# A transformer block with routed experts: where the experts' steps that no tile fills stand

## The reference

```python
logits = einsum('bsh,eh->bse', h, gate_w) + expert_bias
weights = softmax(logits)
top_w, top_i = top_k(weights, 2)
top_w = top_w / (sum(top_w) + 1e-6)
for e in range(8):
    g = gelu(einsum('bsh,ih->bsi', h, w_up[e]))     # 256 -> 1024
    y = einsum('bsi,hi->bsh', g, w_down[e])         # 1024 -> 256
    out = out + sparse_w[..., e:e + 1] * y
out = layernorm(out) + h
x = x + gb * out
```

## Time and profile before

| | |
|---|---|
| median of three runs | 1329.73 us |
| profiled execution | 1329.79 us, span 1328.1 us |
| busy in the span: PE, DVE, ACT, POOL | 1115.8, 795.6, 643.0, 867.1 us |
| share of the chain that ended last: PE, issue, DVE, DMA, POOL | 30%, 2%, 2%, 1%, 1% |
| DMA queue of SP and ACT | 137.59 MB, 37.8% of 16 engines |
| DMA queue of POOL | 28.11 MB, 11.3% of 16 engines |

### The profile page before, as it was taken

One profiled execution on the slowest core, in us unless ns is written; L12 is line 12 of the kernel. 1 busy time (PEld: TensorE's weight loads), 2 busy tenths in 40 slices (PEclk: granted clock), 3 DMA queues, 4 the chain that ended last, 5 costly groups with the idle time before them and its releaser, 6 DMA issues. The chain is left out here.

```text
span 1328.1 us, 30712 instructions
## 1 busy us (share of the span) xinstructions
PE 1115.8 (84%) x11290; PEld 889.4 (67%) x11291; DVE 795.6 (60%) x2048; ACT 643.0 (48%) x913; POOL 867.1 (65%) x959
## 2 busy tenths in 40 slices
PE   4569999998999989989899813699999999999900
PEld 3346776777777767767677611588888888888800
DVE  4445668567685676756868359455555555555557
ACT  3447776775767767767677402122222222222212
POOL 2266597676875777758855437566666666666656
PEclk9779999999999999999999855799999999999965
DMA  8778674753548526564361245134344344242364
GB/s 289 205 204 182 219 180 116 177 125 102 150 113 200 126 97 144 136 173 136 91 128 65 96 159 159 33 50 110 57 98 110 45 110 110 47 107 48 45 161 131
DMA packets 122892, 167.14 MB, mean 126 GB/s; under 512 B 13048, under 2 KB 99320, under 8 KB 122784
## 3 DMA queue, kind: packets, MB, share of 16 engines
q1 hardware_dynamic: 103200, 137.59, 37.8%
q0 software_dynamic: 19584, 28.11, 11.3%
HBM read 105.22 MB, written 60.44 MB: 125 GB/s over the span
## 5 line engine op out<-in xcount | busy, mean ns | idle before, releaser
L927 DVE CUSTOM_DVE_ANT_0 b_sn<-b_ps_s,s_tile 128x512 f32<-128x512 f32 x512 | 341.5, 688 | 202.6 <-PE b_ps_s L1056 199.5
L869 ACT ACTIVATE b_pt<-b_ps_t 128x1024 f32<-128x1024 f32 x256 | 259.5, 1017 | 89.1 <-PE b_ps_t L1070 89.1
L1070 PE MATMUL b_ps_t<-s_ident,b_sn 128*128 128x128 f32 x2048 | 274.3, 277 | 9.8 <-POOL b_sn L760 8.1
L1070 PEld LDWEIGHTS b_ps_t<-s_ident,b_sn 128*128 128x128 f32 x2048 | 243.3, 143 | 48.1 <-issue 19.0
L760 POOL TENSOR_SCALAR b_sn<-b_sn,b_mn 128x512 f32<-128x512 f32 x256 | 175.3, 696 | 116.5 <-DVE b_mn L927 115.5
L1656 ACT ACTIVATE d_g<-d_ps_u 128x512 f32<-128x512 f32 x156 | 92.7, 598 | 315.1 <-PE d_ps_u L1769 308.6
L861 ACT ACTIVATE b_sn<-b_sn,b_mn 128x512 f32<-128x512 f32 x256 | 182.4, 721 | 101.1 <-DVE b_mn L927 94.1
L1056 PE MATMUL b_ps_s<-s_ks,s_qs 96*128 96x512 bf16 x512 | 181.9, 391 | 27.4 <-DVE b_mn L927 20.5
L1769 PE MATMUL d_ps_u<-d_xp,k_wu 128*128 128x256 bf16 x1776 | 201.9, 274 | 0.0
L1784 PE MATMUL d_ps_y<-k_wd,d_gp 128*128 128x256 bf16 x1776 | 199.9, 273 | 0.0
L1769 PEld LDWEIGHTS d_ps_u<-d_xp,k_wu 128*128 128x128 bf16 x1776 | 173.7, 98 | 21.7 <-issue 0.2
(11 more groups left out here) (198 smaller groups left out, 1219.7 us busy)
## 6 DMA issues: line engine op xcount, KB each, us to landing
w_parts<-b_w_split SPq DMA_DIRECT2D x32, 512.0 KB, 3.6
splits<-s_parts SPq DMA_DIRECT2D x32, 384.0 KB, 3.2
s_qs<-splits SPq DMA_DIRECT2D x96, 128.0 KB, 6.0
s_ks<-splits SPq DMA_DIRECT2D x96, 128.0 KB, 7.6
b_w_raw<-in_w_up_t SPq DMA_DIRECT2D x16, 512.0 KB, 10.6
b_w_raw<-in_w_down_t SPq DMA_DIRECT2D x16, 512.0 KB, 6.9
k_wu<-w_parts SPq DMA_DIRECT2D x8, 1024.0 KB
k_wd<-w_parts SPq DMA_DIRECT2D x8, 1024.0 KB
```

The lines of the kernel that those rows point to most:

```text
L869: act.activation(pt[:, m, 2 * pair:2 * pair + 2, :], ps_t[:, 2 * pair:2 * pair + 2, :], ACT.Exp).then_inc(exped, 1)
L927: dve.tensor_tensor_reduce(sn[:, n % 2, t, :], ps_s[:, t % 2, :], ahead.tile[:, n, at:at + S], -1.0, BIG, ALU.add, ALU.min, mn[:, n % 2, t ...
L1070: mm = pe.transpose(ps_t[:, j, t * P:(t + 1) * P], sn[:, m, t, j * P:(j + 1) * P], ident[:, :])
```

## The change

A turn is five steps. The first turns end in an empty step each, until there are no empty steps left; after that the filled ones go on without a gap. `empty` is 39 less the filled tiles. A place moves up by 256 for each empty step ahead of it: its tile divided by four (`STRIDE - 1`), at most `empty`. The same is done for `kept.filled`; the tables of slot and count of loads are looked up by the step less the empty steps before it, and a step is marked as empty where it is the fifth of a turn whose number is under `empty`. SP now waits for the scatters of all 39 steps before it reads the sums. In `up` TensorE waits, bank by bank, for gelu of the step before, which an empty step in between no longer covers.

```diff
+STRIDE = 5
+TURNS = -(-TABLE // STRIDE)
...
+            pool.iota(ints[:, AT_TURN:AT_MARK], pattern=[[1, TURNS], [0, STRIDE]], base=0, channel_multiplier=0).then_inc(pool_step, 1)
+            pool.iota(ints[:, AT_MARK:], pattern=[[1, TURNS], [-100, STRIDE]], base=100 * (STRIDE - 1), channel_multiplier=0).then_inc(pool_step, 1)
...
             rows = kept.rows[:, :, :].rearrange("p k t -> p (k t)")
+            turn = ((STRIDE - 1) * ROWS).bit_length() - 1
+            dve.tensor_scalar(empty[:, :], filled[:, NE - 1:NE], -1.0, float(RUN_TILES), ALU.mult, ALU.add)
+            link(dve.tensor_scalar(turn_u[:, 0:2 * NT], rows, turn, None, ALU.logical_shift_right))
+            link(dve.tensor_copy(turn_f[:, 0:2 * NT], turn_u[:, 0:2 * NT]))
+            link(dve.tensor_scalar(turn_f[:, 0:2 * NT], turn_f[:, 0:2 * NT], empty[:, :], float(ROWS), ALU.min, ALU.mult))
+            link(dve.tensor_tensor(turn_f[:, 0:2 * NT], turn_f[:, 0:2 * NT], places[:, :, :].rearrange("p k t -> p (k t)"), ALU.add))
+            link(dve.tensor_copy(rows, turn_f[:, 0:2 * NT]))
...
-            dve.tensor_scalar(kept.scattered[:, :], filled[:, NE - 1:NE], 16.0 * TT, None, ALU.mult)
-            link(dve.tensor_scalar(kept.filled[:, :], filled[:, :], 1.0, None, ALU.add))
+            of_expert = slice(2 * NT, 2 * NT + NE)
+            link(dve.tensor_copy(filled_u[:, :], filled[:, :]))
+            link(dve.tensor_scalar(turn_u[:, of_expert], filled_u[:, :], (STRIDE - 1).bit_length() - 1, None, ALU.logical_shift_right))
+            link(dve.tensor_copy(turn_f[:, of_expert], turn_u[:, of_expert]))
+            link(dve.tensor_scalar(turn_f[:, of_expert], turn_f[:, of_expert], empty[:, :], 1.0, ALU.min, ALU.add))
+            dve.tensor_tensor(kept.filled[:, :], filled[:, :], turn_f[:, of_expert], ALU.add)
             link(dve.tensor_scalar(last_tile[:, :], filled[:, NE - 1:NE], -1.0, None, ALU.add))
-            link(dve.tensor_scalar(index[:, :], iota_t, last_tile[:, :], None, ALU.min))
+            link(dve.tensor_scalar(index[:, :], turns, empty[:, :], None, ALU.min))
+            link(dve.tensor_tensor(index[:, :], iota_t, index[:, :], ALU.subtract))
+            link(dve.tensor_scalar(index[:, :], index[:, :], last_tile[:, :], None, ALU.min))
...
-            link(dve.tensor_scalar(scaled[:, :, 0], iota_t, last_tile[:, :], float(SPARE), ALU.is_gt, ALU.mult))
+            link(dve.tensor_scalar(scaled[:, :, 0], marks, empty[:, :], float(SPARE), ALU.is_lt, ALU.mult))
...
-            sp.wait_ge(y_out, sp.value_load(kept.scattered[0:1, 0:1], min_val=16, max_val=16 * TT * MAX_TILES))
+            sp.wait_ge(y_out, 16 * TT * RUN_TILES)
...
                 pe.wait_ge(kept.w_ready[slot], loaded)
                 for j in range(NIC):
+                    if j % 2 == 0:
+
+                        at_least(pe, gelued, (t - 1) * BANKS + j // 2 + 1)
```

More of the change, by code:

```diff
@@ L1207 @@
 SPARE = 2
+STRIDE = 5
+TURNS = -(-TABLE // STRIDE)
+assert (2 * STEPS - 1) // (STRIDE - 1) >= NE - 1
 SLOT, LOADED = range(2)
@@ L1231, in __init__ @@
         self.places = sb("places", [P, TABLE, 2, TT], U32)
-        self.scattered = sb("scattered", [P, 1], I32)
         self.tiles = sb("tiles", [P, 2, TABLE], I32)
@@ L1256, in route @@
         up_to = sb("up_to", [P, NE, NE])
-        ints = sb("ints", [P, NE + STEPS + TABLE + P], I32)
-        nums = sb("nums", [P, NE + STEPS + TABLE + P])
+        CONSTS = NE + STEPS + TABLE + P + 2 * TURNS * STRIDE
+        ints = sb("ints", [P, CONSTS], I32)
+        nums = sb("nums", [P, CONSTS])
         swing = sb("swing", [P, NE])
@@ L1277, in route @@
         last_tile = sb("last_tile", [P, 1])
+        empty = sb("empty", [P, 1])
+        turn_u = sb("turn_u", [P, 2 * NT + NE], U32)
+        turn_f = sb("turn_f", [P, 2 * NT + NE])
+        filled_u = sb("filled_u", [P, NE], U32)
         index = sb("index", [P, TABLE])
@@ L1293, in route @@
         ps_r = ctx.enter_context(nc.psum_tensor("c_ps_r", [P, 2, NT, 2 * NE], F32))
-        iota_e, steps, iota_t, iota_p = (nums[:, 0:NE], nums[:, NE:NE + STEPS], nums[:, NE + STEPS:NE + STEPS + TABLE],
-                                         nums[:, NE + STEPS + TABLE:])
+        AT_P = NE + STEPS + TABLE
+        AT_TURN = AT_P + P
+        AT_MARK = AT_TURN + TURNS * STRIDE
+        iota_e, steps, iota_t, iota_p = nums[:, 0:NE], nums[:, NE:NE + STEPS], nums[:, NE + STEPS:AT_P], nums[:, AT_P:AT_TURN]
+        turns, marks = nums[:, AT_TURN:AT_TURN + TABLE], nums[:, AT_MARK:AT_MARK + TABLE]
         consts_ready, pool_step = sem("consts_ready"), sem("pool_step")
@@ L1326, in _ @@
                 pool.iota(ints[:, at:at + n], pattern=[[step, n]], base=0, channel_multiplier=0).then_inc(pool_step, 1)
+            pool.iota(ints[:, AT_TURN:AT_MARK], pattern=[[1, TURNS], [0, STRIDE]], base=0, channel_multiplier=0).then_inc(pool_step, 1)
+            pool.iota(ints[:, AT_MARK:], pattern=[[1, TURNS], [-100, STRIDE]], base=100 * (STRIDE - 1), channel_multiplier=0).then_inc(pool_step, 1)
             pool.iota(place_in[:, :], pattern=[[0, 1]], base=1, channel_multiplier=1).then_inc(pool_step, 1)
-            pool.wait_ge(pool_step, 7)
+            pool.wait_ge(pool_step, 9)
             for i in range(TT):
@@ L1558, in _ @@
                 sp.wait_ge(kept.w_ready[e % 2], 32 * (e // 2))
-                sp.wait_ge(downed, sp.value_load(kept.filled[0:1, e - 2:e - 1], min_val=1, max_val=MAX_TILES + 1))
+                sp.wait_ge(downed, sp.value_load(kept.filled[0:1, e - 2:e - 1], min_val=1, max_val=RUN_TILES + 1))
                 load_weights(sp, kept, w_parts, e)
```

## The result

The changed kernel takes 1338.69 us (median of six runs, 1336.23 to 1341.74) against 1329.45 of the kernel before (six runs, 1326.35 to 1332.06): ratio 1.0074, 95% interval 1.0058 to 1.0091. It is slower by 9 us, where the forecast had 3.3 slower; 1338.7 lies inside the stated range of 1327.5 to 1339.5, near its upper end.

What follows compares the result with a forecast made beforehand. TensorE sets the pace at 11.27 us a step, with POOL's fixed-order round close at 10.91. 1.2 + 15.0 + 0.7 - 3.6 - 8.0 - 2.0 = +3.3 on 1329.79 gives 1333.1 us, range 1327.5 to 1339.5.

Steps and rivals of the forecast that it cites:

- the norm's head start: Last stage's layer norm: POOL's power no longer waits behind the empty steps, -8.0 us, and its adds move, -2.0.
- Routing, +1.2: Before the experts: six small VectorE instructions ahead of `placed`, covered by nothing, cost 1.2 us (0.9 to 1.6).
- The four waits, 0: In each `up`: waits for gelu of the step before cost 0, less than 1.5 us over 37 steps.
- Step 4: First empty step: TensorE waits for tile 3's results, 4 us more (3 to 6), not counted because of step 9.
- Step 9, S(11) at 964.30: Second empty step: TensorE stands 8 us for tile 11's load; `up` of step 11 starts at 964.30, +15.0 us.
- late landings: POOL's scatters in the experts' stage: one wait for a late landing beside expert 2's weights, +0.7 us (0 to 2).
- It has the 27 steps to catch up: Filled steps after the second empty one: POOL, 5 us behind, regains 0.36 us a step over 27 steps.
- the tail's first term: From the last product to the last tile's rows in memory: 7.5 us instead of 11.1, -3.6 (-2 to -4).
- The tail's second and third term, -10.0: After the read-back: VectorE gets POOL's power without waiting, -8.0 us; POOL's adds fall beside the moments, -2.0.
- that POOL becomes the pace: Rival in the experts' stage: POOL's round is 11.27 us, the lag is not made up, 1338.2 us; chance 0.17.
- The rule that VectorE's casts hold POOL's DMAs: Rival beside the empty steps: four casts of 0.43 in each of two rounds, 3.5 us, 1336.6; chance 0.05.
- The rival of two short stops: Both empty steps cost 4 us, the clock never falls, 1325.4 us; chance 0.15 together with a clock that stays up.

Runs made afterwards that it cites:

- b_waits: The kernel before plus only the change's four waits in each `up` on gelu of the step before; ratio 1.0013 to the kernel before.
- a_onegate: The changed kernel with one gate DMA per tile instead of two; ratio 1.0021 to the kernel before.
- a_late: The changed kernel, but SyncE sends for the next expert's weights only when the last scatter using the buffer has landed; ratio 1.0015 to the kernel before.
- a_small: The changed kernel with weight loads of experts 2 to 7 cut to 32 columns instead of 2 MB each; ratio 1.0044 to the kernel before.
- b_onegate: The kernel before with one gate DMA per tile instead of two; ratio 0.9990 to the kernel before.
- a_keep: a_late plus 32 TensorE transposes behind raising `upped` in each empty step; ratio 1.0042 to the kernel before.
- b_root: The kernel before with POOL's power replaced by a square root on ScalarE and a reciprocal on VectorE; ratio 0.9986 to the kernel before.

## Why the prediction came out as it did, step by step

The time lies in the stated range, 5.6 us above the forecast of 1333.1. The account of the two ends (the stop at step 9, the norm's head start) was right; what lies between them, POOL's recovery, was not.

- **Routing, +1.2**: right, +1.3 (from the places' cast to the first shift 1.53 instead of 0.23).
- **The four waits, 0**: 1.75 in the profile of `b_waits`. The rows of 5.40 were too coarse: an error of 0.05 a step doesn't show in them.
- **Step 4, "4 us more, which does not count"**: it cost 5 to 5.6, and the restart on the low clock 1.2 to 1.5. It did not count here, since POOL's load came later still; but `a_onegate` shows that it would have, with a faster POOL.
- **Step 9, S(11) at 964.30**: it came at 968.61. Of the 4.3: scatter(3) 0.7 later (the first turn is 0.9 later in this execution, the scatter 0.2 earlier behind it), 2.5 in the four rounds (46.13 instead of 43.64, the wait of 2.78 for the landing), 0.4 to the load, 1.1 in its landing (3.82, where I had taken the 2.76 of the quiet start), -0.4 in the restart. I had allowed 0.7 for late landings. The mechanism and the place were right, and the clock fell there. That it falls needs no such long stop: it fell at step 4's 4.0 us too, and in `a_late` at 2.0.
- **"It has the 27 steps to catch up"**: this is the step that failed. I took a late landing for a single event, where each of six loads of weights meets a scatter once POOL lags. Six waits took 13.0 us; 33 rounds regained 0.34 each, 11 in all, against TensorE's 11.27 a step. So **the tail's first term**, -3.6, was +0.3; `a_late` and `a_small` have it at -3.8 and -3.9, and B and C there (+15.2 and -3.8 for `a_late`) are close to the forecast's +15.7 and -3.6. B is made up otherwise, though: stops of 4.0, 2.0 and 4.2, each with a restart on the low clock, in place of a single long one.
- **The tail's second and third term, -10.0**: -9.9.
- **The rivals.** The first, that POOL becomes the pace, is what happened, by another way than a longer round: the round stayed 10.93, and the waits for landings did it. That its 1338.2 is so near the 1338.7 is in part luck, since it came from another cause. The rule that VectorE's casts hold POOL's DMAs had 3.5 us for the two rounds beside empty steps. The rounds right behind scatter(3) and scatter(8) took 11.52 and 11.41, 1.1 over 10.91 together, with single calls of POOL longer beside the casts (1.33 and 1.08 where 0.97 is usual): something of it may be in these, not the 3.5. The rival of two short stops was priced too low: 14 us for both, not 8, so that even a free POOL does not make the change faster (`a_onegate` is 6.0 slower than `b_onegate`).

The balance: 14 us are to be had at the end, and moving the empty steps brings 10 of them (14 where POOL catches up), but each empty step costs TensorE 7 in the middle.

## What to carry to other kernels

A step that does nothing on the bounding engine still costs it a handshake through the others and a restart; where it stands last, only what is queued behind it pays, and moving that (here one power and two adds) is cheaper than moving the step. Before shifting one engine against another, read how much the second slowest regains a step, and what its transfers will meet at the new phase: a transfer that used to fall between two others can fall on one every time. And a free stretch on an engine is only free if no semaphore that others need is raised behind it.

## What the runs showed of the chip that I had not expected

- The granted clock fell between 3.8 and 4.3 us behind TensorE's last matmul at 893.66 (1.00 until 897.50, mean 0.56 in the next half us), against the 4.8 of the earlier trace rows; in `a_late` it fell as a stop of 2.02 us ended (mean 0.69 in 934.50 to 935.00, the restart at 934.58); in `a_keep` it stayed up at one of 2.07 and fell some 1.2 us behind the next, of 2.08. So a stop of 2 us was at times enough. The first 48 products behind such stops took 6.5 to 7.9 us instead of 5.4.
- Two loads of 1 MB beside it hold a scatter of 128 rows from 3.88 to 7.75 us until it is landed.
- VectorE's products beside POOL's adds lost about as much time as the adds took: 4.6 for 4.26 (`b_root`).
